# The decay mixes of blocks 1 to 7: modulation loaded onto all partitions, products moved from VectorE to ScalarE and GpSimd

## The reference

```python
ctx = causal_ema(x, tau_ctx)
wg = sigmoid(concat([x, ctx]) @ Wg.T + bg)
gated = x * wg
h1 = gelu(x @ Wn1.T + bn1)
mod = 0.5 + sigmoid(h1 @ Wn2.T + bn2)                 # (B, T, 16): one column per decay d
traces = vmap(lambda tau, m: causal_ema(gated * m[..., None], tau))(tau_raws, moveaxis(mod, -1, 0))
temporal = einsum('dbtc,dc->btc', traces, softmax(blend, axis=0))
gate = sigmoid(temporal @ Wtemp.T + btemp)
soma = gelu(x @ Wsoma.T + bsoma)
out = layernorm((soma * gate) @ Wout.T)
```

## Time and profile before

| what | value |
| --- | --- |
| median of three runs | 2878.78 us |
| the profiled execution: its time | 2876.17 us |
| its span, first to last instruction | 2874.4 us |
| PE busy | 2818.4 us, 98% |
| VectorE busy | 1846.4 us, 64% |
| ScalarE busy | 1390.2 us, 48% |
| GpSimd busy | 1233.3 us, 43% |
| mean granted PE clock | 0.993 of 2.4 GHz |
| moved by DMA | 201.22 MB, mean 70 GB/s |

### The profile page before, as it was taken

The page is one execution under the profiler, slowest core; times in us unless marked ns, Lnnn a source line. Parts: engine busy times, 40 slices in busy tenths (PEclk is TensorE's granted clock), DMA queues, the critical chain, the costliest instruction groups (busy, mean ns, idle before and its releaser), DMA issues.

```text
span 2874.4 us, 36550 instructions
## 1 busy us (share of the span) xinstructions
PE 2818.4 (98%) x13018; PEld 2331.4 (81%) x13018; DVE 1846.4 (64%) x3017; ACT 1390.2 (48%) x2408; POOL 1233.3 (43%) x950
## 2 busy tenths in 40 slices
PE   8699999999999999999999999999999999999999
PEld 5488888788888888888788888888888888888888
DVE  8699778867777766556865666655776563333443
ACT  4544555465336633454534553344643473333445
POOL 5256434643463445433554345542455333333333
PEclk9899999999999999999999999999999999999999
DMA  4133332322112311111311131111221122111231
GB/s 150 60 116 99 90 94 78 111 92 93 57 48 68 115 48 50 48 50 48 94 45 48 56 92 45 48 45 52 74 70 57 47 87 63 50 45 44 72 92 57
DMA packets 85573, 201.22 MB, mean 70 GB/s; under 512 B 10312, under 2 KB 27152, under 8 KB 85392
## 3 DMA queue, kind: packets, MB, share of 16 engines
q1 hardware_dynamic: 82256, 190.38, 21.5%
q0 software_dynamic: 2560, 8.39, 1.0%
q10 hardware_dynamic: 576, 0.11, 0.0%
HBM read 190.75 MB, written 8.09 MB: 69 GB/s over the span
## 4 chain that ended last, share of the span: by engine, by line
PE 88%; DVE 7%; issue 2%; ACT 2%; DMA 1%; SPq 0%; DVEq 0%; ACTq 0%
PE bank L557 19%; PE bank L559 19%; PE bank L558 19%; PE ps_out L557 9%; PE ps_out L559 9%; PE ps_out L558 9%; DVE trace L1075 2%; DVE w_lo L1145 2%; DVE trace L1067 1%; PE bank L550 1%; PE bank L631 1%; DVE hid L1169 0%; DMA stat<-mod_rows 0%; ACT L867 0%; PE bank L679 0%
## 5 line engine op out<-in xcount | busy, mean ns | idle before, releaser
L1308 POOL TENSOR_TENSOR hid_lo<-hid,hid_hi 128x512 fp32r<-128x512 f32 x640 | 865.6, 1353 | 1581.2 <-ACT hid_hi L954 1580.9
L557 PE MATMUL bank<-res_lo,w_hi 128*128 128x512 f32 x2432 | 963.3, 396 | 6.2 <-DVE res_lo L1160 3.3
L559 PE MATMUL bank<-res_hi,w_hi 128*128 128x512 f32 x2432 | 953.1, 392 | 0.0
L558 PE MATMUL bank<-res_hi,w_lo 128*128 128x512 f32 x2432 | 951.9, 391 | 0.0
L1169 DVE TENSOR_TENSOR hid<-hid,bank 128x512 f32<-128x512 f32 x576 | 393.3, 683 | 540.8 <-PE bank L559 512.8
L926 ACT ACTIVATE hid<-bank 128x512 f32<-128x512 f32 x576 | 344.0, 597 | 663.9 <-PE bank L559 662.8
L1145 DVE TENSOR_TENSOR w_lo<-w_raw,w_hi 128x768 fp32r<-128x768 f32 (+2 forms) x520 | 513.5, 989 | 177.9 <-ACT w_hi L895 139.6
L895 ACT ACTIVATE w_hi<-w_raw 128x768 fp32r<-128x768 f32 x392 | 331.4, 845 | 540.0 <-PE ps_out L559 513.4
L559 PEld LDWEIGHTS bank<-res_hi,w_hi 128*128 128x128 f32 x2432 | 458.3, 188 | 103.3
L557 PEld LDWEIGHTS bank<-res_lo,w_hi 128*128 128x128 f32 x2432 | 458.8, 189 | 100.5 <-issue 6.7
L558 PEld LDWEIGHTS bank<-res_hi,w_lo 128*128 128x128 f32 x2432 | 459.3, 189 | 86.4
(11 more groups left out here) (179 smaller groups left out, 1624.4 us busy)
## 6 DMA issues: line engine op xcount, KB each, us to landing
w_raw<-in_chunks SPq DMA_DIRECT2D x392, 384.0 KB
w_raw<-in_head_chunks SPq DMA_DIRECT2D x64, 224.0 KB
x_in<-in_xT SPq DMA_DIRECT2D x16, 256.0 KB, 3.6
pre_x<-in_xT SPq DMA_DIRECT2D x14, 256.0 KB, 7.0
soma_rows<-pre_soma SPq DMA_DIRECT2D x14, 256.0 KB, 2.0
soma<-soma_rows SPq DMA_DIRECT2D x14, 256.0 KB, 3.1
out_yT<-acc SPq DMA_DIRECT2D x7, 512.0 KB, 2.8
acc<-in_sidew SPq DMA_DIRECT2D x2, 512.0 KB, 7.1
```

Source lines behind the costliest of these rows:

```text
L557: mm(out, wh, xl, start=start and i == 0, stop=False, skip_group_check=not lone)
L558: mm(out, wl, xh, start=False, stop=False, skip_group_check=not lone)
L559: last = mm(out, wh, xh, start=False, stop=end, skip_group_check=not lone)
L1308: nc.gpsimd.tensor_tensor(hid_lo[i % DEPTH][:], hid[i % 3][:], f(hid_hi[i % DEPTH][:]), ALU.subtract).then_inc(s_hlo, 1)
```

## The change

For blocks 1 to 7 mod no longer goes through PE. GpSimd scales the tanh in the pre parts (the store waits for it, pre_pool). Each row of mod_rows is then read from HBM by a DMA that repeats it on all 128 partitions, two rows at a time, 256 KB: rows 0 and 1 by SyncE at piece 2 with soma, into temporal; rows 2 to 9 by four DMAs on ScalarE's queue at piece 5, behind the gate's tanh, into the four split tiles (mod_on) that are free then; rows 10 to 15 by three more, after the weighing of decays 7, 9 and 11. ScalarE weighs (weigh d: gated * bl[d] into the trace, two activations), from piece 6 on, two pieces ahead of the scan; GpSimd multiplies by the modulation row (mul d, a piece ahead of the scan) besides its add; VectorE only scans. Traces rotate over four buffers, the fourth being ema. Stages "mod_hi", "modpair" and the PE mixes of these blocks go. In order(), a mix piece of blocks 1 to 7 costs 2.5 and piece 5 costs 0. The new semaphores s_on and pre_pool and the call of pre in GpSimd's loop are left out below.

```diff
@@ -81,10 +81,10 @@
     if 7 <= j < 7 + ND:
-        return 2.1
+        return 2.5 if b else 2.1
...
-    return {0: 1.3, 5: 1.0, 34: 1.7, 36: 1.4, 42: 1.5, 24: 0.0, 25: 0.0, 29: 0.0, 37: 0.0, 43: 0.0}.get(j, 0.7)
+    return {0: 1.3, 5: 1.0 if b == 0 else 0.0, 34: 1.7, 36: 1.4, 42: 1.5, 24: 0.0, 25: 0.0, 29: 0.0, 37: 0.0, 43: 0.0}.get(j, 0.7)
@@ -252,13 +252,26 @@
+
+FROM_DRAM = {
+    "act": [f"weigh{d}" for d in range(ND)],
+    "pool": ["mul0", "mul1", "mul2"] + [x for d in range(2, ND + 1) for x in [f"add{d - 1}"] + [f"mul{d + 1}"] * (d + 1 < ND)],
+}
...
-    if 1 <= b <= PRE and stages is not SIDE_DVE:
-        return [x for x in stages if x not in ("h1", "soma", "mod")]
+    if 1 <= b <= PRE:
+        if stages is SIDE_POOL:
+            return FROM_DRAM["pool"]
+        gone = ("h1", "soma", "mod", "mod_hi", "modpair")
+        left = [x for x in stages if x not in gone and not x.startswith("mix" if stages is SIDE_PE else "mul")]
+        if stages is SIDE_ACT:
+            k = left.index("alpha") + 1
+            left[k:k] = FROM_DRAM["act"]
+        return left
@@ -340,7 +353,11 @@
         soma_rows = nc.dram_tensor("soma_rows", (NPRE, P, DH * S), fp32, kind="Internal").ap()
-        mod_rows = nc.dram_tensor("mod_rows", (NPRE, ND, S), fp32, kind="Internal").ap()
+        mod_rows = nc.dram_tensor("mod_rows", (NPRE, ND * S), fp32, kind="Internal").ap()
+        mod_on = [[t[s][:].bitcast(fp32) for t in (one_hi, one_lo, two_hi, two_lo)] for s in range(BB)]
+        ring = [trace[s] + [ema[s]] for s in range(BB)]
@@ -487,8 +505,8 @@
                 elif k == 3:
-                    sp.wait_ge(pre_act, 3 * u + 3)
-                    sp.dma_start(mod_rows[u], pre_mod[u % 3][0:ND, :]).then_inc(s_store[u % 3], 16)
+                    sp.wait_ge(pre_pool, u + 1)
+                    sp.dma_start(mod_rows[u].rearrange("(d t) -> d t", d=ND), pre_mod[u % 3][0:ND, :]).then_inc(s_store[u % 3], 16)
@@ -497,7 +515,9 @@
                 sp.dma_start(soma[s][:].rearrange("p h t -> p (h t)"), soma_rows[u]).then_inc(s_back[s], 16)
-                sp.dma_start(stat[s][0:ND, :], mod_rows[u]).then_inc(s_back[s], 16)
+                sp.dma_start(temporal[s][:].rearrange("p h t -> p (h t)"),
+                             mod_rows[u, 0:2 * S].partition_broadcast(P)).then_inc(s_on[s][4], 16)
@@ -578,7 +598,7 @@
                 ahead = 1 <= b <= PRE
-                if ahead and j in (2, 3, 4):
+                if ahead and (j in (2, 3, 4) or 7 <= j < 7 + ND):
@@ -799,6 +819,29 @@
+            def spread(b, s, i):
+                u = (b - 1) * BB + s
+                act.wait_ge(s_store[u % 3], 32 * (u // 3 + 1))
+                act.dma_start(mod_on[s][(i - 1) % 4].rearrange("p h t -> p (h t)"),
+                              mod_rows[u, 2 * i * S:2 * (i + 1) * S].partition_broadcast(P)).then_inc(s_on[s][(i - 1) % 4], 16)
+            def weigh(b, s, d):
+                if d >= ND:
+                    return
+                if d == 0:
+                    act.wait_ge(l_dve[s], dve_at(s, b, "gated"))
+                elif d == 4:
+                    act.wait_ge(l_dve[s], dve_at(s, b, "scan0"))
+                elif d > 4:
+                    act.wait_ge(l_pool[s], pool_at(s, b, f"add{d - 4}"))
+                for h in range(DH):
+                    last = activate(ring[s][d % 4][:, h, :], gated[s][:, h, :], ACT.Copy, scale=bl[:, h, d:d + 1])
+                last.then_inc(l_act[s], 1)
+                if d in (7, 9, 11):
+                    spread(b, s, (d + 3) // 2)
@@ -833,12 +876,18 @@
                     last.then_inc(l_act[s], 1)
+                    if b:
+                        for i in range(1, 5):
+                            spread(b, s, i)
...
+                elif 6 <= j < 7 + ND and b:
+                    for d in (0, 1) if j == 6 else (j - 5,):
+                        weigh(b, s, d)
@@ -1041,10 +1090,9 @@
                 elif j == 5:
-                    if 1 <= b <= PRE:
-                        dve.wait_ge(s_back[s], 32 * b)
-                    else:
-                        dve.wait_ge(l_act[s], act_at(s, b, "mod"))
+                    if b:
+                        return
+                    dve.wait_ge(l_act[s], act_at(s, b, "mod"))
@@ -1055,7 +1103,17 @@
                     d = j - 7
-                    tr = trace[s][d % 3]
+                    tr = ring[s][d % 4] if b else trace[s][d % 3]
+                    if b:
+                        if d == 0:
+                            dve.wait_ge(l_act[s], act_at(s, b, "alpha"))
+                        dve.wait_ge(l_pool[s], pool_at(s, b, f"mul{max(d, 1)}"))
+                        for h in range(DH):
+                            last = V.tensor_tensor_scan((temporal[s] if d == 0 else tr)[:, h, :],
+                                                        ps[:, S + d:S + d + 1].broadcast_to([P, S]),
+                                                        tr[:, h, :], 0.0, ALU.mult, ALU.add)
+                        last.then_inc(l_dve[s], 1)
+                        return
@@ -1069,8 +1127,8 @@
                     if d == 0:
-                        dve.wait_ge(l_act[s if b else 0], act_at(s if b else 0, b, "alpha"))
-                    decay = ps[:, S + d:S + d + 1] if b else lead_alpha[:, d:d + 1]
+                        dve.wait_ge(l_act[0], act_at(0, b, "alpha"))
+                    decay = lead_alpha[:, d:d + 1]
@@ -1080,6 +1138,8 @@
                     dve.wait_ge(l_act[s], act_at(s, b, "tgate"))
+                    if b:
+                        dve.wait_ge(s_back[s], 16 * b)
@@ -1295,13 +1355,30 @@
                         in_offset=bass.IndirectOffsetOnAxis(ap=pen_row[:, q:q + 1], axis=0)).then_inc(s_pen[s], 16)
-                elif 9 <= j < 8 + ND:
+                if 9 <= j < 8 + ND:
...
-                    nc.gpsimd.tensor_tensor(temporal[s][:], temporal[s][:], trace[s][d % 3][:],
+                    nc.gpsimd.tensor_tensor(temporal[s][:], temporal[s][:], (ring[s][d % 4] if b else trace[s][d % 3])[:],
                                             ALU.add).then_inc(l_pool[s], 1)
+                if b and 6 <= j < 6 + ND:
+                    d = j - 6
+                    i = d // 2
+                    pool.wait_ge(l_act[s], act_at(s, b, f"weigh{d}"))
+                    if d == 0:
+                        pool.wait_ge(s_on[s][4], 16 * b)
+                    elif d % 2 == 0:
+                        k = (i - 1) % 4
+                        pool.wait_ge(s_on[s][k], 16 * ((2 if k < 3 else 1) * (b - 1) + (i - 1) // 4 + 1))
+                    row = (mod_on[s][(i - 1) % 4] if i else temporal[s][:]).rearrange("p h t -> p (h t)")[:, d % 2 * S:(d % 2 + 1) * S]
+                    nc.gpsimd.tensor_tensor(ring[s][d % 4][:], ring[s][d % 4][:], row.unsqueeze(1).broadcast_to([P, DH, S]),
+                                            ALU.mult).then_inc(l_pool[s], 1)
+            def pre(u, k):
+                if k == 3:
+                    pool.wait_ge(pre_act, 3 * u + 3)
+                    TS(pre_mod[u % 3][0:ND, :], pre_mod[u % 3][0:ND, :], 0.5, 1.0, ALU.mult, ALU.add).then_inc(pre_pool, 1)
```

More of the change, by code:

```diff
@@ L414, in residual_stack_kernel @@
         s_back = [sem(f"pre_back{s}") for s in range(BB)]
+        s_on = [[sem(f"mod_in{s}_{i}") for i in range(5)] for s in range(BB)]
         s_y = [sem(f"y_out{i}") for i in range(NACC)]
@@ L418, in residual_stack_kernel @@
         l_pe, l_act, l_dve, l_pool = ([sem(f"lane{s}_{n}") for s in range(BB)] for n in ("pe", "act", "dve", "pool"))
-        pre_pe, pre_act = sem("pre_pe"), sem("pre_act")
+        pre_pe, pre_act, pre_pool = sem("pre_pe"), sem("pre_act"), sem("pre_pool")
         s_wlo, s_whi, s_rhi, s_rlo = sem("w_lo"), sem("w_hi"), sem("res_hi"), sem("res_lo")
@@ L1313, in _ @@
                     side(*x[1:])
+                elif x[0] == "pre":
+                    pre(*x[1:])
                 elif x[0] == "setup":
```

## The result

| | time, us | interval or spread |
| --- | --- | --- |
| before, median of 7 runs | 2878.26 | 2875.59 to 2880.15 |
| changed, median of 7 runs | 2893.51 | 2885.98 to 2899.63 |
| ratio | 1.0051 | 1.0041 to 1.0060 |
| changed, profiled execution | 2895.99 | span 2894.1, granted clock 0.988 |

The forecast was 2861 and faster; the time lies inside the range, near its end, and on the wrong side of before. Two executions of the study far outside the others, 3450.7 us of before and 10033.7 of bo_apart3, are left out of the medians and ratios.

The account below looks back on a forecast made before the run. TensorE's own work was taken as the bound; -27 - 3 - 3 + 2 + 1 + 5 + 8 = -17 us against the profiled 2876.2 gave 2859, with the runs' median 2.6 higher 2861.8, written as 2861; range 2836 to 2895.

Parts of the forecast that it names:

- Part 1: TensorE in blocks 1 to 7: 224 mix matmuls go, 0.12 us saved each, -27 us.
- Parts 2 and 3: TensorE's waits at the mixes go, -3 us (0 to -7); VectorE, relieved, causes fewer TensorE idles, -3 (0 to -9).
- Part 4: ScalarE gains 448 activations and 98 load issues, making the next silu 2.7 us late, mostly within slack; +2 us (0 to +14).
- part 6: GpSimd's 224 added products contend with VectorE for SBUF: +5 us drift, +8 kept turns, +1 for block 0's small products.
- Part 5: The broadcast loads of modulation rows, 256 KB in about 3 us each, are hidden before their use; 0 us.
- rival A: All slack holds: no new stall, and the old VectorE waits go; 2838 us, chance 0.22.
- The kept turns: GpSimd keeps SBUF instead of alternating with VectorE's w_lo, 3 in 29, some 15 of 158 places; +8 us (0 to +30).
- forecast: The main case, a time from 2846 to 2872 us, chance 0.44.
- C: GpSimd keeps the port, starving w_lo in every step with mix and cut; 2912 us, chance 0.18; sign: w_lo mean above 2.
- D: Slow broadcasts: 22 us for four loads, products wait, 98 us more, 2959; chance 0.04; sign: add or product waits for a load.
- B: Stalls for slots: drift and kept turns double and eat the 27 us; 2878, chance 0.12; sign: PE idle above 45 us.

Follow-up runs that it names:

- bo_apart3: b_order with pieces 38 and 44 held back until three steps after 36 and 42; 2885.9 us, ratio 1.0033.
- f_old: The changed kernel with both old side costs (2.1 a mix piece, 1.0 for piece 5), so before's order; 2876.3 us, ratio 0.9996.
- f_old_seh: The changed kernel with old side costs, scan0 a piece later, rows 0 and 1 loaded at piece 0, no pieces 6 to 22 in head steps; 2845.0 us.
- b_order: The kernel before with both new side costs (2.5 a mix piece, 0 for piece 5) and nothing else; 2895.6 us, ratio 1.0063.
- e_early: The changed kernel with SyncE's load of rows 0 and 1 at piece 0 instead of piece 2; 2888.3 us, ratio 1.0040.
- f_old_se: The changed kernel with old side costs, scan0 a piece later and rows 0 and 1 loaded at piece 0; 2864.8 us, ratio 0.9955.
- e_gather: The changed kernel with GpSimd's indirect loads of the head's rows emitted four chunks later; 2904.0 us, ratio 1.0098.
- b_gather: The kernel before with GpSimd's indirect loads of the head's rows emitted four chunks later; 2880.3 us, ratio 1.0011.

## Why the prediction was wrong

**Part 1, right.** f_old has before's order. In the quiet stretches (steps 16 to 48, 192 to 240, 296 to 340 and 352 to 440) it is 13.9 us shorter, and 98 mixes have gone from them: 0.14 us each, near the 0.12 of the prediction. The whole fits: with the idle of 190 to 2290 us the same as before, 17.5 and 17.4, f_old_seh's profiled execution is 30 us shorter (2845.86 against 2876.17). Parts 2 and 3 (-3 each) were not measured apart.

**Part 4, right in size, wrong in its place.** Two activations cost 0.9 us a mix, four issues 1.7 us. ScalarE's busy total was 1551 against the 1640 forecast, of which 42 were issues, and busy time doesn't count those. It told not at the next silu but at a lane's start: GpSimd's first product waited 50.3 us for the weighing, in eight places. Taken out, the weighing is worth 3 us at the most; +2 had been taken.

**The step that failed first is the one that isn't there.** The sum has no term for the order. I used the changed side costs in part 6 only, for the pace ("mixes come in about 0.82 of the steps"), and took it that the pieces otherwise stay where they were. They moved: scan0 of one lane, which had stood behind the other lane's x1 in VectorE's queue, came ahead of it, and in lane 1 the matmul that needs x1 came one step behind it instead of two or three. That is +19 us in the kernel before (b_order) and 17 in the changed one (f_old; 16 by the ratios). The time of a step in which two queues meet is not in their total loads, which is why the busy times could come out within 6% of the forecast.

**Part 5, "0", was wrong.** SyncE's load was to be hidden by "gate, tanh, gated and weigh, above 5 us". A load lands in 3.4 to 5.2 us by the medians, 4.4 for these:

```profile
temporal<-mod_rows SPq DMA_DIRECT2D x14, 256.0 KB, 4.4
two_lo<-mod_rows ACTq DMA_DIRECT2D x14, 256.0 KB, 5.2
```

but the issue was late. In the changed order piece 2 stands at step 180, one before piece 6, and no longer two as in before's; on SyncE's queue it stood behind a weight load that waited for its buffer, which the w_lo of 945.05 us frees:

```profile
946.50 0.33 SPq L497 DMA_DIRECT2D w_raw<-in_chunks  x1
946.93 0.38 SPq L517 DMA_DIRECT2D soma<-soma_rows  x1
947.35 0.43 SPq L519 DMA_DIRECT2D temporal<-mod_rows  x1
```

The tanh came at 947.64 and the two weighings from 949.60 to 951.29, while the product started with the landing, 6.1 us after the issue, at 953.55. So these loads were slow as well as late: in the six places where GpSimd waited for rows 0 and 1 they took 5.0 to 6.2 us, in the eight others 3.7 to 4.6. The waits were 39.8 us in all:

```profile
POOL trace L1375 <- DMA temporal<-mod_rows: 39.8, 6, 8.1
DVE temporal L1112 <- POOL trace L1375: 37.3, 13, 7.3
```

The early load is worth 5 us at the most (e_early), all loads together 12 (9 by the ratios). This too is mostly the order's work: in f_old the same wait is 7.3 us in two places. And part 5 asked only whether the row is late, not who stands behind the wait. scan0 waits for product 1, a wait on two other engines that the kernel before did not have, with the other lane's x1 queued behind it: late scan0 and early load are 25 us in the new order, 11 in the old. That wait is in the diff, one line, and the prediction doesn't name it.

**Part 6, mechanism right, size and place wrong.** The dense part of block 1 was to drift by 5 us; it lost none (TensorE 100% from 200 to 300 us, as rival A had it). The heads, where the prediction had counted 4.1 of 2.8 us and then let 5 and 8 us stand for everything, cost 20 (f_old_seh against f_old_se) in the old order and 8 in the new. The kept turns are not 3 in 29 spread over 158 places at 0 to 2 us each. Counting a w_lo (128 x 768) that starts under a GpSimd operation with the next at most 0.1 us behind, VectorE went next in 106 of 113 places of the changed kernel and in 29 of 32 of before; the seven others all start 1.2 to 2.6 us behind an indirect load, and each lasts till GpSimd's next gap. In before that gap came after seven operations; with a product more in each mix it came after thirteen. GpSimd's product in all costs 44 us of the changed kernel, against the 14 taken.

**The rivals.** The two chances of the sum don't follow from their parts: forecast and A make 0.66 for faster, C and D 0.22 for slower, not 0.68 and 0.20. That 2893.5 lies in the range at all is luck, since the upper end of 2895 is half of C's loss, a price that was not paid. A (2838) was right for the dense steps. B's account, slots lost in stalls, is the nearest in kind; its sign for a failure, idle above 45 us, was met. C's price was not paid: w_lo's mean is 1.22 us, not above 2. D's sign, products that wait for a load, appeared at about a tenth of its price (9 to 12 of 98 us). What the forecast lacked was any case in which pieces that the change doesn't touch move.

Put together from the runs, in the order of taking them away: the new costs 17, late start and late load 11, the heads 20. These 48 us (46 by the ratios) lie between the 2893.5 of the change and the 2845.0 of f_old_seh, which is 31 us under its own before, where parts 1 to 3 alone had 33.

## What to carry to other kernels

A number in a planner is an edit of the whole program: print the old and the new order and compare, for each pair of producer and consumer on different engines, how many steps lie between and what stands ahead of the producer in its queue, before costing anything else. When a result is moved from one engine to a chain of three, look up what is queued behind the first wait for it, on its engine; the wait belongs a piece later or the work behind it ahead. And test a planner's numbers alone: here two settings, each free by itself, cost 19 us together.

## What the runs showed of the hardware

GpSimd and VectorE took turns in 106 of 113 places of the changed kernel and in 29 of 32 of before. The exception is sharp: behind an indirect load on GpSimd's queue GpSimd kept on until its own next gap, and a w_lo stood for 15.96, 13.10 and 9.39 us (513, 1406, 2105 us). Where the indirect load was issued four chunks later, the long w_lo moved with it (9.41 us at 528 in e_gather, 4.71 at 523.5 in b_gather, each behind a moved load). The Trainium skill (SBUF — State Buffer, Who interferes with whom) has the exclusion but no order of turns; why an indirect load changes it no run here shows.

A broadcast of one 2 KB piece of HBM to all partitions, 256 KB, lands in 3.4 to 5.2 us by the medians, against 3.3 for a plain 256 KB load (soma); a further one on ScalarE's queue costs that queue 0.33 to 0.45 us.
